# Moving query features to head groups with 128-row transfers, and turning the maxima with one transpose

## The reference, cut to what matters

```python
x = x + tanh(g_xattn[0]) * L0_xattn(ctx, layernorm(x), ...)   # differential attention, 32 half heads of 8
x = x + tanh(g_ffn[0])   * L0_ffn(layernorm(x), ...)          # router, top 3 of 8 zones, gelu
x = x + tanh(g_xattn[1]) * L1_xattn(layernorm(x), ctx, ctx)   # 16 heads of 16, one Wq for q, k and v
x = x + tanh(g_ffn[1])   * L1_ffn(layernorm(x), ...)          # silu gate, int weights
# x is 2 x 1024 x 256, ctx is 2 x 77 x 256; both attentions:
q = Q @ Wq (+ bq); k = K @ Wk; v = V @ Wv; att = softmax(q k^T * scale); out = att @ v
```

## Time and profile before

| what | value |
|---|---|
| median of 3 runs | 671.64 us (671.02 to 672.87) |
| the profiled execution | 671.35 us, span 669.6 us |
| PE busy | 608.3 us, 91% |
| DVE, ACT, POOL busy | 57%, 54%, 22% |
| transfers SP to `QG` from `QH`, `QL` | 144 of 64 KB, issue 0.59 us each |
| transfers POOL to `QG` | 48 of 64 KB, issue 0.50 us each |

### The profile page before, as it was taken

How to read it: one execution, slowest core, us unless ns; L and a number is a source line. 1 busy time by engine, 2 the same in 40 slices (tenths; PEclk the granted TensorE clock), 3 DMA queues, 4 the chain that set the end, 5 groups by cost and what they waited for, 6 DMA issues and landing times.

```text
span 669.6 us, 11648 instructions
## 1 busy us (share of the span) xinstructions
PE 608.3 (91%) x4364; PEld 503.0 (75%) x4364; DVE 384.5 (57%) x813; ACT 361.6 (54%) x615; POOL 148.2 (22%) x218
## 2 busy tenths in 40 slices
PE   2688888898899999999999999999778998999998
PEld 2565555554599899999999888899656776878887
DVE  6668676887753524434555434534486663656654
ACT  4345757686765746546557435535675433443421
POOL 9716265354630000000000000000564210210000
PEclk9789999999999999999999999999999998999999
DMA  7302120222030030300312340020132100000000
GB/s 226 107 12 88 35 62 8 49 51 97 32 126 1 10 117 1 118 9 1 126 25 72 80 142 2 2 95 2 44 99 65 35 1 0 34 1 22 12 33 31
DMA packets 22551, 34.76 MB, mean 52 GB/s; under 512 B 4704, under 2 KB 13280, under 8 KB 22496
## 3 DMA queue, kind: packets, MB, share of 16 engines
q1 hardware_dynamic: 20224, 30.51, 14.7%
q0 software_dynamic: 1984, 3.44, 2.2%
q10 hardware_dynamic: 288, 0.07, 0.0%
HBM read 18.93 MB, written 2.10 MB: 31 GB/s over the span
## 4 chain that ended last, share of the span: by engine, by line
PE 73%; DVE 10%; ACT 5%; issue 4%; POOL 3%; DMA 1%; ACTq 0%; DVEq 0%; POOLq 0%
PE PV L1259 21%; PE SC L1287 21%; PE SC L1259 9%; PE PV L1278 4%; PE AUX L1259 4%; DVE NM L1134 3%; PE SC L1406 3%; PE AUX L1368 3%; PE PV L1287 2%; PE AUX L1287 2%; DVE O L1142 2%; ACT PB L906 2%; ACT XN L851 1%; PE AUX L1326 1%; POOL RSTD L716 1%
## 5 line engine op out<-in xcount | busy, mean ns | idle before, releaser
L992 DVE TENSOR_TENSOR HL<-HF,HH 128x512 fp32r<-128x512 f32 x96 | 67.2, 700 | 154.6 <-ACT HH L948 154.4
L906 ACT ACTIVATE PB<-SC 77x1024 f32<-77x1024 f32 x96 | 95.2, 1014 | 50.1 <-PE SC L1406 49.8
L1287 PE MATMUL SC<-WBH,HL 128*128 128x256 f32 x384 | 108.7, 283 | 0.0
L1287 PE MATMUL SC<-WBL,HH 128*128 128x256 f32 x384 | 108.6, 283 | 0.0
L1287 PE MATMUL SC<-WBH,HH 128*128 128x256 f32 x384 | 108.6, 283 | 0.0
L948 ACT ACTIVATE HH<-PV 128x512 fp32r<-128x512 f32 x96 | 57.3, 596 | 72.1 <-PE SC L1287 72.1
L943 ACT ACTIVATE HF<-PV 128x512 f32<-128x512 f32 x96 | 57.3, 597 | 54.7 <-PE PV L1259 52.7
L716 POOL TENSOR_TENSOR RSTD<-RSTD,NHALF 128x4 f32<-128x4 f32 x16 | 17.8, 1115 | 291.5 <-DVE RSTD L1066 291.4
L1259 PE MATMUL PV<-XH,WAH 128*128 128x512 f32 x192 | 77.6, 404 | 1.0 <-DVE O L1142 1.0
L1287 PEld LDWEIGHTS SC<-WBL,HH 128*128 128x128 f32 x384 | 72.7, 189 | 3.9
L1287 PEld LDWEIGHTS SC<-WBH,HH 128*128 128x128 f32 x384 | 72.5, 189 | 4.0 <-DVE HL L992 0.3
(11 more groups left out here) (254 smaller groups left out, 1228.7 us busy)
## 6 DMA issues: line engine op xcount, KB each, us to landing
QG<-QH SPq DMA_DIRECT2D x96, 64.0 KB, 2.0
WSA<-in_wa SPq DMA_DIRECT2D x6, 1024.0 KB, 4.8
WSB<-in_wb SPq DMA_DIRECT2D x12, 512.0 KB, 6.4
QG<-QL SPq DMA_DIRECT2D x48, 64.0 KB, 2.0
X<-in_x SPq DMA_DIRECT2D x4, 512.0 KB, 6.0
QG<-QH POOLq DMA_DIRECT2D x32, 64.0 KB, 2.3
out_x<-X SPq DMA_DIRECT2D x8, 256.0 KB, 2.1
QG<-QL POOLq DMA_DIRECT2D x16, 64.0 KB, 2.3
```

The costliest lines, as they stand in the source:

```text
L906: act.activation(probs(n)[0:S, :, :], scores(n)[0:S, :, :], ACT.Exp, scale=SCALE[a]).then_inc(exp_done, 1)
L992: return dve.tensor_tensor(dst, raw, hi.bitcast(F32), ALU.subtract)
L1287: ins = pe.matmul(ps[:, D * (t % 2):D * (t % 2 + 1)], lhs[:, block], rhs, start=first and t == 2 * i and n == 0, stop=last and t == 2 * i ...
```

## The change

Wq of both layers is laid out on the host so that row p = 4r + g of a half holds feature r of group g (`by_row`; the bias too). One transfer then takes all 128 rows of `QH` or `QL` to 32 partitions by 4 groups. A half takes 3 transfers of 256 KB, all issued by SP. `BOTH`, POOL's share and its semaphores are gone. The key path and the value path of layer 1 use the same Wq and undo the order as they read it: ACT fills `WDH` and POOL fills `WDL` in four instructions of 384 columns with a step of four elements in the source, and the value matmuls read `WQ1H` and `WQ1L` with that step.

`NM` is laid out head by token block, so that a half's maxima are 64 (32) adjacent columns. One transpose gives 64 (32) rows by 128 tokens, ACT copies that, and the SP transfers take 16 (8) rows of 512 bytes to a group's 4 (2) partitions.

```diff
-                    for r in range(2 if n in BOTH else 4):
-                        for q, src in enumerate((QH, QL, QH)):
-                            sp.dma_start(QG[n % 2][32 * q:32 * q + 32, 4 * c + r, :].bitcast(F32),
-                                         src[32 * r:32 * r + 32, c, :].bitcast(F32)).then_inc(q_moved[n % 2][c], 16)
+                    for q, src in enumerate((QH, QL, QH)):
+                        sp.dma_start(QG[n % 2][32 * q:32 * q + 32, G // KC * c:G // KC * (c + 1), :].bitcast(F32),
+                                     src[:, c, :].bitcast(F32)).then_inc(q_moved[n % 2][c], 16)
...
+        def by_group(raw, c, h):
+
+            return (raw[:, c, P * h:P * (h + 1)].rearrange("p (r g) -> p g r", g=G // KC)
+                    .unsqueeze(2).to_broadcast([P, G // KC, 3, 32]))
...
+            def move_maxima(queries, a, g, at_g):
+
+                return sp.dma_start(queries[ROWS:ROWS + NS[a], g, :].bitcast(F32),
+                                    NMT[at_g:at_g + NS[a] * TT, :].bitcast(F32))
...
-                elif kind == "q_move" and J * step[1] + step[2] in BOTH:
...
-                    for r in range(2, 4):
-                        for q, src in enumerate((QH, QL, QH)):
-                            pool.dma_start(QG[n % 2][32 * q:32 * q + 32, 4 * c + r, :].bitcast(F32),
...
-                    pool.wait_ge(split_hi, 6)
+                    pool.wait_ge(split_hi, 9)
                     for c in range(KC):
-                        lo_part(WDL[:, c, :, :, :],
-                                WQ1R[:, c, :].rearrange("p (g r) -> p g r", r=32).unsqueeze(2).to_broadcast([P, G, 3, 32]),
-                                WDH[:, c, :, :, :]).then_inc(split1_done, 1)
+                        for h in range(KC):
+                            gs = slice(G // KC * h, G // KC * (h + 1))
+                            lo_part(WDL[:, c, gs, :, :], by_group(WQ1R, c, h), WDH[:, c, gs, :, :]).then_inc(split1_done, 1)
...
-                    dup_hi(WQ1R)
+                    for c in range(KC):
+                        for h in range(KC):
+                            act.activation(WDH[:, c, G // KC * h:G // KC * (h + 1), :, :], by_group(WQ1R, c, h),
+                                           copy).then_inc(split_hi, 1)
...
-                    act.activation(NMT[32 * c:32 * c + n_heads, :], bank(step + (0,))[0:n_heads, :], copy).then_inc(frees(step + (0,)), 1)
+                    rows = HEADS[a] // KC * TT
+                    act.activation(NMT[64 * c:64 * c + rows, :], bank(step + (0,))[0:rows, 0:P], copy).then_inc(frees(step + (0,)), 1)
...
+                            vh, vl = (tuple(w[:, c, :].rearrange("p (k r g) -> p k g r", k=KC, g=G // KC)
+                                            for c in range(KC)) for w in (vh, vl))
...
-                    for t in range(TT):
-                        ins = pe.transpose(ps[0:n_heads, P * t:P * (t + 1)],
-                                           NM[:, (J * a + j) % 2, t, n_heads * c:n_heads * (c + 1)], ident[:, :])
+                    turn_maxima(ps, NM[:, (J * a + j) % 2, n_heads * c:n_heads * (c + 1), :]).then_inc(aux_ready, 1)
...
+            def turn_maxima(ps, maxima):
+
+                rows = maxima.shape[1] * TT
+                return pe.transpose(ps[0:rows, 0:P], maxima.rearrange("p h t -> p (h t)"), ident[:, :])
...
+    def by_row(w):
+        return w.reshape(-1, KC, G // KC, 32).transpose(0, 1, 3, 2).reshape(w.shape)
```

More of the change, by code:

```diff
@@ L58 @@
 WIDE = 64
-BOTH = (0, 1, 6, 7)
 def weave(main, side):
@@ L396, in flamingo @@
         SG = [at(f"SG{i}", [P, NT], F32, wq_at + 4096 + 2048 * i) for i in range(2)]
-        NM = place("NM", [P, 2, TT, HEADS[0]], F32)
-        NMT = place("NMT", [P, NT], F32R)
+        NM = place("NM", [P, 2, HEADS[0], TT], F32)
+        NMT = place("NMT", [P, P], F32R)
         ident = place("ident", [P, P], F32)
@@ L535, in query_moved @@
         def query_moved(eng, n, c):
-            eng.wait_ge(q_moved[n % 2][c], 16 * sum(6 if m in BOTH else 12 for m in range(n % 2, n + 1, 2)))
-            if n in BOTH:
-                eng.wait_ge(pool_moved[n][c], 16 * 6)
+            eng.wait_ge(q_moved[n % 2][c], 16 * 3 * (n // 2 + 1))
+        def by_group(raw, c, h):
+            return (raw[:, c, P * h:P * (h + 1)].rearrange("p (r g) -> p g r", g=G // KC)
+                    .unsqueeze(2).to_broadcast([P, G // KC, 3, 32]))
         def ffn_half(i, h):
@@ L630, in _ @@
                     for g in range(G // KC):
[L631 to L633 removed]
+                        move_maxima(QG[n % 2], a, G // KC * c + g,
+                                    64 * c + NS[a] * TT * g).then_inc(m_moved[n % 2][G // KC * c + g], 16)
                 elif kind == "negpart":
@@ L894, in _ @@
                     filled(act, key)
-                    act.activation(NMT[at_p:at_p + 8, :], bank(key)[0:8, :], copy).then_inc(frees(key), 1)
+                    act.activation(NMT[at_p:at_p + 32, :], bank(key)[0:32, 0:P], copy).then_inc(frees(key), 1)
                 elif kind == "attend":
@@ L1133, in _ @@
                     filled(dve, key)
-                    dve.tensor_reduce(NM[:, n % 2, t, h:h + k], bank(key)[:, 0:k * S].rearrange("p (h n) -> p h n", h=k),
+                    dve.tensor_reduce(NM[:, n % 2, h:h + k, t], bank(key)[:, 0:k * S].rearrange("p (h n) -> p h n", h=k),
                                       AX_X, ALU.max, negate=True).then_inc(frees(key), 1)
@@ L1343, in _ @@
                         cols = slice((i - 3) * S, (i - 2) * S)
-                        ins = product(ps[0:S, 0:D], [(CH[:, c, cols], CL[:, c, cols], vh[:, c, :], vl[:, c, :])
-                                                     for c in range(KC)])
+                        if a == 0:
+                            vh, vl = (tuple(w[:, c, :] for c in range(KC)) for w in (vh, vl))
+                        else:
+                            vh, vl = (tuple(w[:, c, :].rearrange("p (k r g) -> p k g r", k=KC, g=G // KC)
+                                            for c in range(KC)) for w in (vh, vl))
+                        ins = product(ps[0:S, 0:D], [(CH[:, c, cols], CL[:, c, cols], vh[c], vl[c]) for c in range(KC)])
                     ins.then_inc(aux_ready, 1)
@@ L1517 @@
         "wa": inputs["L0_ffn_Wa"], "wb": inputs["L0_ffn_Wb"],
-        "wq1": inputs["L1_xattn_Wq"], "bq": bq,
-        "bq_c": bq.reshape(KC, P).T, "bq_g": np.tile(bq.reshape(G, 32).T, (3, 1)),
+        "wq1": by_row(np.asarray(inputs["L1_xattn_Wq"])), "bq": bq,
+        "bq_c": by_row(bq[None]).reshape(KC, P).T, "bq_g": np.tile(bq.reshape(G, 32).T, (3, 1)),
         "wo": inputs["L1_xattn_Wo"], "bo": inputs["L1_xattn_bo"],
```

21 lines of the change are left out of this document (4 added, 17 removed).

## The result

The changed kernel takes 680.83 us (median of 5, 679.36 to 681.25) against 671.64 us: the ratio is 1.0127, with a 95% interval of 1.0111 to 1.0144. It is 1.3% slower, where 666.2 us was forecast and 670.5 us was the upper end. The profiled execution took 681.25 us with a span of 679.4 us, 9.8 us more than before.

The account below looks back on a forecast made before the run. PE was taken as the bound, most fully from 179 to 476 us, with the order of steps limiting other stretches. Gains of 6.7 us less losses of 1.4 us gave net 5.3 us: 666.2 us, range 663.0 to 670.5.

Parts of the forecast that it names:

- Transfers of the query features: Tile 0's first half at the start: 768 KB at 211 GB/s land by 26.4 us, before `KA`; cost nothing.
- Rival E: One queue is slow at the start, costing 3.8 us: 670.1 us; chance 0.05.
- POOL's issues: Near 482 us: without six POOL issues the bias addition ends before DVE's `WGL` split; gain 1.3 us, bounds 0 to 1.8.
- Turning the maxima: Fewer transposes and a narrower copy: gains of 1.2 us at the start, 2.0 and 1.1 in attention, 1.1 in zones.
- sum for the zones: Zone stretch, four steps: three copy waits at 0.29 us plus 0.26 us of transposes, 1.1 us gained.
- list of signs: Profile signs of being right; among them, PE's three waits for the maxima copy shrink by 0.3 us each.
- Rival C: Order of steps swallows the gains in layer 0's attention and at POOL's addition; 1.4 us left, 670.2 us; chance 0.13.
- The two attention terms: Maxima turning in attention: 2.0 us gained over layer 0's 7 steps, 1.1 us over layer 1's 4 steps.
- rival D: More gain: full attention and split gains, step nearly free, 1.6 us from a vanished half-clock stretch; 662.0 us; chance 0.08.
- Reading weights with a step: Layer 1's key and value path: POOL's `WDL` fills lose 1.0 us, the 12 value matmuls 0.4 us.

Follow-up runs that it names:

- narrow_two_queues: Changed kernel with its weight layout, but each half again in 12 transfers of 32 rows, on SP and POOL: 673.22 us, ratio 1.0000.
- maxima_split_7: maxima_alone with POOL's share of the query transfers for tiles 0, 1 and 7 only, tile 6 all on SP: 670.25 us, ratio 0.9964.
- maxima_alone: Kernel before with only the maxima's turning changed (one transpose, narrow copy, 512-byte pieces); query transfers and weights as before: 669.12 us, ratio 0.9953; again 669.30 us, 0.9950.
- pairs_64: Changed kernel with a half in six SP transfers of 64 rows to 32 partitions by 2, weights read with an 8-byte step: 672.85 us, ratio 0.9999.
- four_plain: maxima_alone with four fills each for WDH and WDL, as in the changed kernel, but reading without a step: 669.06 us.

## Why the prediction was wrong, by its own steps

**Transfers of the query features: the step that failed.** "With the 211 GB/s that SP and POOL reached together in this stretch" the half was to land 1 us before `KA` was ready, so "I cost this at nothing; `KA` on DVE hides it". The rate was carried over from 32-row transfers to another shape. The new shape moves 129 GB/s with all 16 DMA engines busy. Rival E had this case ("one queue is slow", 3.8 us) but took an unshared queue for the only reason, gave it 0.05, and with "only the first half of tile 0 is waited for" priced it at one place. The waits before had no item for the others since each transfer landed in 2.0 us. The cover ended in these places:

- 29.09 us, first half of tile 0: 1.5 us late.
- 58.09 us, tile 1: PE waits 1.54 us for a transfer issued at 50.99. The maxima's four transfers, issued from 59.01, stand in SP's queue behind the three of the tile's other half, the last of which landed at 64.0 us, and PE waits 2.00 us more, to 64.49, where it waited 0.69 us before.
- 526.86 us, tile 7: PE waits 1.72 us for a transfer issued near 520.
- Each idle stretch is followed by a stretch at the lower of the two clock levels. From 58 to 66 us the clock was 0.75, from 520 to 530 us 0.81:

```profile
58.00:66.00 8.00, 5.91 (x32) 3.74 (x33) 3.40 (x6) 2.03 (x3) 1.93 (x3) 0.75 0.63 75
520.00:530.00 10.00, 5.78 (x69) 3.89 (x59) 2.25 (x4) 5.75 (x10) 0.00 (x0) 0.81 0.84 123
```

From 39.8 to 98 us the clock accounts for the 3.5 us of added busy time: 46.90 x 0.90 and 43.44 x 0.97 are both about 42 us of work at full clock. The added idle time there is 4.3 us. That the low clock follows from the waits wasn't tried apart. *narrow_two_queues*, in which a half lands in time again (2.2 us, first maxima at 27.75 us), gives 8.5 us back.

**POOL's issues.** Right as a row, wrong as a gain: the split took 0.96 us for 2.79, but *maxima_split_7* shows no time from it. Where the time goes instead wasn't traced. The 1.3 us should have been 0.

**Turning the maxima.** The instructions came as forecast. The `negpart` transpose takes 0.37 us, the stretch to 39.8 us is the forecast 1.2 us shorter, and the zones are 1.2 us shorter where 1.1 was forecast. The three waits for the copy there did not shrink, 2.5 us in sum for 2.4: PE reaches each of them earlier by the transposes that it no longer makes, as the forecast's own sum for the zones had it and its list of signs had not. ACT's copy, of 64 or 32 rows, in the changed kernel:

```profile
L885 ACT ACTIVATE NMT<-AUX 64x128 fp32r<-64x128 f32 x7 | 1.9, 266 | 1.8 <-PE AUX L1259 1.8
L885 ACT ACTIVATE NMT<-AUX 32x128 fp32r<-32x128 f32 x6 | 1.6, 261 | 6.2 <-PE AUX L1259 6.1
```

Its price was 5.4 us in sum; *maxima_alone* is 3.5 and 3.6 us faster than the kernel before by the medians of its two calls (672.59 - 669.12, 672.88 - 669.30). Rival C has it that the rest only lengthened waits. The profiles don't show that: PE was idle for 61.3 us before (669.6 - 608.3), for 62.4 us in *maxima_alone* and for 60.1 us in its second profile. What they show is a lower clock. One place of half clock is gone, from 564 us on, worth about 8 x 0.21 = 1.7 us of work. Those 8 us before, then in *maxima_alone*:

```profile
564.00:572.00 8.00, 8.00 (x56) 0.79 0.01 4
```

```profile
564.00:572.00 8.00, 8.00 (x71) 1.00 0.01 2
```

But other places came. Two stretches of *maxima_alone*, where the earlier trace rows has 0.64 and 1.00:

```profile
27.60:39.50 11.90, 9.70 (x28) 6.99 (x29) 7.89 (x19) 3.80 (x8) 1.17 (x2) 0.50 0.11 32
...
476.00:500.00 24.00, 18.06 (x219) 13.00 (x220) 18.27 (x35) 18.99 (x26) 15.80 (x18) 0.93 0.36 100
```

Over all executions of both calls the median granted clock is 0.982 before and 0.977 in *maxima_alone*. As an estimate, 0.005 of 670 us is about 3 us of PE's work, more than the 1.9 us that are missing from the 5.4. The two attention terms, 2.0 and 1.1 us, were too large or the clock took part of them back. So rival D's hope, that the second half-clock stretch goes away, came out the other way. Whether the lighter work brings the low clock about, and how much time it costs, wasn't tried apart. One profile doesn't settle where the clock falls: the two of this same kernel differ in it (476 to 500 us at 0.93 and 0.86) and are 1.8 us apart in span.

**Reading weights with a step.** Costed at 1.0 and 0.4 us. `WDL` takes 4.65 us for four, 1.05 us more than before, so the first is right. The 12 value matmuls of layer 1 are 0.23 us apart at full clock where they were 0.12: 12 x 0.11 = 1.3 us, near the upper bound; this term was mis-sized by 0.9 us. ACT's `WDH` fills take 3.23 us where one took 1.49; I had 0.2 to 0.5 us more, and it is 1.7 us more, off the path. Rows of the timeline of the changed kernel, for POOL, PE and ACT; then the same of *pairs_64*, with its step of 8 bytes; then of *four_plain*, with none, for POOL and ACT:

```profile
93.28 4.65 POOL L695 TENSOR_TENSOR WDL<-WQ1R,WDH 128x384 fp32r<-128x384 f32 x4
...
119.40 0.41 PE L1253 MATMUL AUX<-WQ1L,CH 128*77 128x256 f32 x1
119.63 0.41 PE L1253 MATMUL AUX<-WQ1H,CL 128*77 128x256 f32 x1
...
86.94 3.23 ACT L824 ACTIVATE WDH<-WQ1R 128x384 fp32r<-128x384 f32 x4
```

```profile
89.42 3.95 POOL L696 TENSOR_TENSOR WDL<-WQ1R,WDH 128x384 fp32r<-128x384 f32 x4
...
114.23 0.41 PE L1254 MATMUL AUX<-WQ1L,CH 128*77 128x256 f32 x1
114.46 0.41 PE L1254 MATMUL AUX<-WQ1H,CL 128*77 128x256 f32 x1
...
83.08 1.85 ACT L825 ACTIVATE WDH<-WQ1R 128x384 fp32r<-128x384 f32 x4
```

```profile
85.64 3.88 POOL L700 TENSOR_TENSOR WDL<-WQ1R,WDH 128x384 fp32r<-128x384 f32 x4
...
79.30 1.76 ACT L840 ACTIVATE WDH<-WQ1R 128x384 fp32r<-128x384 f32 x4
```

So a step of 16 bytes costs POOL 20% (4.65 for 3.88) and ACT 84% (3.23 for 1.76), a step of 8 bytes next to nothing on either, and PE half its rate at both. The Trainium skill ("GPSIMD Engine Reference", performance pitfalls) sets the edge at more than 8 bytes, and the rows agree; its half as much again is too high here. By the Trainium skill ("SBUF — State Buffer", specifications) two hits in a 16-byte line are enough for full rate. A step of 8 bytes has two, and PE reads it at half rate, so the measurement decides against the page for these matmuls.

**What stays open.** Why 128 rows to 32 partitions by 4 run at 129 GB/s. It is neither the queue, nor the size, nor joined rows, nor the count of destination partitions, nor the rows read, nor several rows to a partition, nor an even share of rows, each taken alone. Theory T joins the last two: if the 16 DMA engines share a transfer's rows evenly, a share of 8 or 4 rows is slow where two or more of them go to one partition. No longer run here contradicts it and none tries it apart; why 96 to 24 by 4 lies between it doesn't say. A wide transfer starts at 369 GB/s and slows within 0.6 us. The second one, issued 0.74 us after the first, would by the first's delay begin only at 22.7 us, as an estimate, so it is hardly a matter of transfers that hinder each other. Slow were 128 to 32 by 4, 128 to 64 by 2 and 64 to 16 by 4; 96 to 24 by 4 and, under load, 64 to 32 by 2 lay between; 128 to 128, 96 to 96 and 96 to 32 by 3 were fast. Of the 4.1 us between *narrow_two_queues* and *maxima_alone*, some 2 us are the two rows of the step; the rest goes with the clock, in the one profile from 489 to 499 us, and whether the layout brings that about wasn't tried.

**Slips of the sum.** 671.64 - 5.3 is 666.3 us and not 666.2, and 1.8 - 0.4 is 1.4 us and not 1.3. Neither matters.

## What to carry to other kernels

A DMA rate belongs to the shape on both sides, not to the bytes: before transfers are merged, measure the new shape, and ask of each reader how long after the issue it starts, since fewer and larger transfers on one queue also land later and hold up small ones behind them. An absent wait proves only that the transfer was short enough. When a change has two parts, run each alone: here the small part was worth 0.5% and the large one cost 1.5%. And before a difference is put down to the clock in one place, look at a second profile of the same kernel.

## What the hardware showed that I had not expected

- The same 256 KB from SBUF to SBUF, on one queue, at 387 GB/s (128 partitions to 128) or 129 (128 to 32 by 4), with the DMA engines shown fully busy in both.
- The wide transfer begins at 369 GB/s and falls to a third of that within 0.6 us, in both tiles looked at. A probe of a shape must outlast this.
- A transfer of 8 KB took 5.43 us behind large ones in its queue, and 1.86 us behind none.
- PE reads its moving operand at half rate with a step of 8 bytes already, 0.23 us for 256 columns in place of 0.12, while ACT (1.85 for 1.76 us) and POOL (3.95 for 3.88 us) don't notice such a step.
